# Row maxima spread through DRAM instead of by four transposes, in a fused cross-attention and feed-forward kernel

## The chip, the cores and the metric

The kernel runs on one core of one Trainium2 chip. The metric is the device time of one execution in microseconds. TensorE (PE) does the matrix products, VectorE (DVE), ScalarE (ACT) and GpSimd (POOL) the elementwise work, and SyncE (SP) starts transfers. Each engine works its own list of instructions in order; semaphores join them.

## The reference

There are B = 16 batches; each has x of 512 rows by 512 and a context c of 77 rows by 512.

```
h    = layernorm(x)
Sim  = (h@w1)[:,None] + (c@w2)[None,:] + (h*w3) @ c.T + b      # 512 x 77
A    = softmax(Sim, over the 77);   hq = A @ c
Batt = softmax(max(Sim, over the 77), over the 512 rows);  hbar = Batt @ h
x    = x + concat(h, hq, h*hq, h*hbar) @ W_qv + b_qv            # W_qv 2048 x 512
y    = layernorm(x) @ W1 + b1                                   # W1 512 x 2048
y    = y + (cos(th)*wr + sin(th)*wi) * 0.1 * wi * sin(th + 0.1*y)
x    = x + relu(y) @ W2 + b2                                    # W2 2048 x 512
```

## The kernel before

Every product is made of three TensorE passes on float32r operands split in a high and a low part (function `three`, lines L509 to L511): high by high, high by low, low by high. ScalarE makes the high part (a cast), VectorE the low part (a subtraction, `low`, L1061).

The work is a software pipeline written out by hand. `attention_first` (the opening) prepares the context products and does the attention of batch 0. Then `body(b, ...)` is run for b = 0 to 15, on each engine its own version. It does the feed-forward part of batch b in 16 steps f = 0 to 15 (one step is one 128-column block of W1 and the matching 128 rows of W2), and in between the attention part of the next batch, n = b + 1. In step f TensorE computes `hidden(b, f)` (12 matmuls into one of two `hid` buffers), and then `second(b, f - 3)` (12 matmuls into `acc`). `hidden(f)` may begin when ScalarE has read the same `hid` buffer (`h2_done` of step f - 2); `second(f - 3)` waits for `act_lo`, the low part that VectorE writes in `relu_low(f - 3)`. For each step ScalarE does `phase_and_hidden` (L866, L869), `relu_high` of the step before (L875) and `sine` (L879); VectorE does `reduce_phase` (L1202, L1204), `sine_term` (L1194) and `relu_low` of the step before (L1208). The pieces of the attention of batch n stand between these, each tied to a value of f. In b = 0 (called `first`) the weights are also split and stored, so each step carries `w1_high`, `w1_low`, `tile_high`, `tile_low` besides; later batches load the split weights again with DMAs from GpSimd.

The attention of batch n, in order: `g_high` and `g_low` (the context scaled by w3 plus w1, split); `spread_high` and `spread_low` (the normalized rows, split); `sim` (TensorE, f = 3, 12 matmuls into `mis[:, 0]`); `sim_bias` (ScalarE); `sim_rows` (four transposes, f = 4); `row_max` (VectorE: `rmax`, 128 x 4, one maximum for each of the 512 rows, f = 4); `spread_max` (TensorE, f = 5, L631: four transposes of a broadcast column of `rmax`, which put all 512 maxima in every partition of `mis[:, 0]`); `whole_max` (VectorE, L1228: their maximum `gmax`, f = 5); `max_exponentials` (ScalarE, L893: the exponentials into `e_bc` and their sum, f = 5); `probabilities`; `whole_prob_turn` (f = 6); `row_mean` (VectorE, L1267, four chunks: the weighted mean of the rows, two chunks at f = 6 and two at f = 7); `context_low` (f = 7); `w0_chunk` (VectorE, L1280, from f = 8), which needs the whole row mean; `hq_hat(0)` on TensorE at f = 9; and after `hidden(11)` the products of the attention, `products`, 16 groups of 12 matmuls whose operands come from `w0_low` and `chunk_low`. In `products` the first matmuls into `acc` wait for `add_first_part` (VectorE, L1304, f = 9), which empties it.

The row statistics of the next batch already go the way by DRAM (`spread_stats`, f = 12): TensorE turns a 128 x 12 tile with one transpose (`turn_stats`, L606), ScalarE copies it from PSUM (L796), SP stores it to `stat_dram` (L352), waits for that, and loads it with a broadcast into `mean_bc` and `e_bc` (L356).

SP's list in `body` is: the context loads at f = 0, the store of batch b - 1 at f = 4, the load of x for the batch after next at f = 6 (`x_load`, L342), `stack_low_in` at f = 7 (two small transfers into `at_s`, needed by `hq_hat(0)`), `turned_load` at f = 11, `spread_stats` at f = 12.

Of the kernel before, what the change touches and what calls it, by code (L numbers as in the profile page):

```python
# [31 lines left out]
ALU = mybir.AluOpType  # L32
# [5 lines left out]
P = 128  # L38
# [12 lines left out]
def xattn_ffn(nc, x, ctx_rows, w_sim, b_sim, W_qv, b_qv, W1, W2, b2, x_turned, ctx_turned, columns, out):  # L51
# [31 lines left out]
    wqx_dram = nc.dram_tensor("wqx_dram", [C, P, 2, D], F32).ap()  # L83
    stat_dram = nc.dram_tensor("stat_dram", [2, 3 * RT, P], F32).ap()
    hqw_dram = nc.dram_tensor("hqw_dram", [B * J, D], F32).ap()

    with ExitStack() as ctx:
# [76 lines left out]
        mv_x = row_x[:, 0:3].rearrange("p k t -> p t k")  # L164
        rmax = sb("rmax", [P, RT])
        rsum = sb("rsum", [P, RT])
        rrec = sb("rrec", [P, RT])
# [38 lines left out]
        exp_done = sem("exp_done"); rsum_done = sem("rsum_done"); rrec_done = sem("rrec_done")  # L206
        prob_done = sem("prob_done"); mbc_done = sem("mbc_done"); gmax_done = sem("gmax_done")
        ebc_done = sem("ebc_done"); erec_done = sem("erec_done"); at_done = sem("at_done")
# [127 lines left out]
        def _(sp):  # L336
# [12 lines left out]
            def spread_stats(n):  # L349
# [5 lines left out]
                for at, dst in ((0, mean_bc[:]), (2 * RT, e_bc[:])):  # L355
                    sp.dma_start(dst, stat_dram[n % 2, at:at + RT].rearrange("(a t) p -> a (t p)", a=1).to_broadcast([P, R])  # L356
                                 ).then_inc(bc_in, 16)

            def rows_in(k):

                need(sp, c_tlo, k - 3)
                m = chunk_rows(k)
                sp.dma_start(c_rows[k % 4][:, :, 0:m], ctx_turned[:, :, k * CR:k * CR + m]).then_inc(c_raw[k % 4], 16)
# [53 lines left out]
            def opening():  # L417
# [7 lines left out]
                rows_in(3)  # L425
                g_load(0, g0_in)
                stack_load(0, hq_raw, hq_tail, ctx_flat, hq0_in)
                rows_in(4)
                sp.dma_start(w2_bc[:], row(w_sim[D:2 * D], P)).then_inc(s_w2, 16)
                sp.dma_start(bsim[:], b_sim.rearrange("(a d) -> a d", a=1).to_broadcast([P, 1])).then_inc(s_bsim, 16)  # L430
                sp.dma_start(bqv_bc[:], row(b_qv, P)).then_inc(s_bqv, 16)
                rows_in(5)
# [33 lines left out]
            def body(b, par, first, last):  # L466
                n, pn = b + 1, 1 - par
                for f in range(FT):
# [10 lines left out]
                    if last:  # L479
                        continue  # L480
                    if f == NA - 3 and not first:
                        stack_low_in(n)
# [23 lines left out]
        def _(pe):  # L506
# [120 lines left out]
            def spread_max(n):  # L627

                pe.wait_ge(rmax_done, n + 1)
                for t in range(RT):  # L630
                    tr = pe.transpose(mis[:, 0, t * P:(t + 1) * P], rmax[:, t:t + 1].to_broadcast([P, P]), ident[:])  # L631
                tr.then_inc(mbc_done, 1)
# [150 lines left out]
        def _(sc):  # L783
# [103 lines left out]
            def row_exponentials(n):  # L887
                sc.wait_ge(shift_done, n + 1)
                nc.scalar.activation(prob[:], prob[:], ACT.Exp).then_inc(exp_done, 1)

            def max_exponentials(n):
                sc.wait_ge(gmax_done, n + 1)
                nc.scalar.activation(e_bc[:], mis[:, 0], ACT.Exp, bias=gmax[:], scale=1.0, accum_out=esum[:]  # L893
                                     ).then_inc(ebc_done, 1)
# [27 lines left out]
            def attention_first():  # L922
# [52 lines left out]
                product_copy(9)  # L975
                g_high(1)

            def body(b, par, first, last):
                n, pn = b + 1, 1 - par
                for f in range(FT):  # L980
# [32 lines left out]
                    if f == 0 and first:  # L1013
                        for c in range(C):
                            spread_high(n, c, pn)
                    if f == 1 and not first:
                        spread_high(n, 2, pn)
                        spread_high(n, 3, pn)
                        g_high(n)
                    if f == (4 if first else 2):  # L1020
                        context_high(n)
                    if f == 3 and not first:
                        sim_bias(n)
                    if f == 5:
                        max_exponentials(n)
# [25 lines left out]
        def _(ve):  # L1051
# [173 lines left out]
            def whole_max(n):  # L1225

                ve.wait_ge(mbc_done, n + 1)
                ve.tensor_reduce(gmax[:], mis[:, 0], AX.X, ALU.max, negate=True).then_inc(gmax_done, 1)  # L1228

# [116 lines left out]
            def attention_first():  # L1346
# [14 lines left out]
                low_part(3)  # L1361
                g_low(0)
                product_add(0)
                low_part(4)
                turned_low(0, 0, 0, full_done, t1_lo)
# [59 lines left out]
            def body(b, par, first, last):  # L1425
                n, pn = b + 1, 1 - par
                for f in range(FT):
# [25 lines left out]
                    if first and f < FT - 3:  # L1453
                        w1_low(f + 3)
                    if f == 0 and not first and not last:
                        scale(n, 0)
                        scale(n, 1)
                    if f == 0 and first:
                        g_low(n)
                        spread_low(n, 0, pn)  # L1460
                        spread_low(n, 1, pn)
                    if f == 1 and not last:
                        sim_column(n)
                        if first:
                            spread_low(n, 2, pn)
                            spread_low(n, 3, pn)
                        else:
                            spread_low(n, 0, pn)
# [12 lines left out]
                    if f == 5 and not last:  # L1481
                        whole_max(n)
                        probabilities(n)
                    if f == 6 and first:
                        prob_low(n)
                    if f == 6 and not last:
                        row_mean_scale(n)
                        row_mean(n, range(0, C // 2))
                    if f == 7 and not last:
                        row_mean(n, range(C // 2, C))  # L1490
                        context_low(n)
                    if f == NA - 2 and not last:
# [3 lines left out]
                    if first:  # L1496
                        for p in splits(f, last)[0:1] if f == NA else splits(f, last):
                            tile_low(p)
                    if f > 0 or not first:
                        relu_low(g - 1, (f - 1) % FT)  # L1500
# [202 lines left out]
```

## Time and profile before

| | us |
|---|---|
| three runs | 1960.26, 1960.32, 1960.84 (median 1960.32) |
| the profiled execution | 1960.47 |
| its span, first to last instruction | 1958.7 |

The view of engines gives busy time and share of the span. The timeline gives for each instruction its start, its duration, and in brackets the idle time before it with what ended that. TensorE's matmuls are pipelined: one lasts 0.39 us by its record, while the next starts about 0.23 us after it, so the distance between two starts is what one costs. The list of waits sums, for pairs of instructions, how long one engine stood idle for another. The granted clock is TensorE's, 1.00 for 2.4 GHz and 0.50 for 1.2 GHz.

### The profile page before, as it was taken

What the parts mean: (1) busy time and instruction counts of PE and PEld (TensorE: products, weight loads), DVE (VectorE), ACT (ScalarE), POOL (GpSimd) and SP (SyncE); (2) the same over time, 40 slices, a digit from 0 to 9 for tenths busy, and PEclk for the clock granted to TensorE, in tenths of its full rate; (3) what the DMA queues carried; (4) which work ended last, traced back from release to release, by engine and by line L of the source; (5) the groups of instructions that cost most, each with busy time, mean ns of one, the idle gap of its engine ahead of it and who ended that gap; (6) DMA issues with size and microseconds to landing.
All of it is one profiled execution on the core that took longest, in us unless ns stands there. A gap on an engine that the chain in (4) does not pass through costs nothing.

```text
span 1958.7 us, 24566 instructions
## 1 busy us (share of the span) xinstructions
PE 1940.7 (99%) x8751; PEld 1591.0 (81%) x8751; DVE 1378.9 (70%) x2377; ACT 985.6 (50%) x1662; POOL 388.9 (20%) x834
## 2 busy tenths in 40 slices
PE   8999999999999999999999999999999999999999
PEld 6778788888888888888888888888888888888887
DVE  7788776767677676776757767676776767767554
ACT  5475635536365363644636355363653636446343
POOL 1123221121211212112121211212112121121210
PEclk9999999999999999999999999999999999999999
DMA  8586847577574875757667475775747757475463
GB/s 258 161 294 233 280 143 232 175 221 221 160 228 143 247 220 165 237 152 223 198 197 223 145 237 163 232 220 159 238 138 240 222 170 232 146 225 183 150 211 123
DMA packets 142151, 393.93 MB, mean 201 GB/s; under 512 B 22100, under 2 KB 35080, under 8 KB 140110
## 3 DMA queue, kind: packets, MB, share of 16 engines
q0 software_dynamic: 83568, 304.29, 50.5%
q1 hardware_dynamic: 58318, 88.04, 14.5%
q8 instruction: 71, 1.16, 0.2%
q14 instruction: 50, 0.41, 0.1%
q10 hardware_dynamic: 144, 0.04, 0.0%
HBM read 351.83 MB, written 38.27 MB: 199 GB/s over the span
## 4 chain that ended last, share of the span: by engine, by line
PE 92%; DVE 3%; ACT 2%; issue 1%; DMA 1%; SPq 1%; DVEq 0%; ACTq 0%
PE acc L509 17%; PE acc L511 17%; PE acc L510 17%; PE hid L509 11%; PE hid L511 11%; PE hid L510 11%; PE mis L595 1%; PE acc L517 1%; PE acc L518 1%; PE mis L517 1%; PE mis L518 1%; PE mis L511 1%; PE mis L509 1%; PE mis L510 1%; DMA ctx_raw<-hqw_dram 0%
## 5 line engine op out<-in xcount | busy, mean ns | idle before, releaser
L509 PE MATMUL hid<-T,w1s 128*128 128x512 f32 x1024 | 403.6, 394 | 4.1 <-ACT h L869 4.0
L509 PE MATMUL acc<-ws,act 128*128 128x512 f32 x1024 | 402.8, 393 | 3.1 <-DVE act L1208 2.3
L510 PE MATMUL hid<-T,w1s 128*128 128x512 f32 x1024 | 399.7, 390 | 0.0
L511 PE MATMUL hid<-T,w1s 128*128 128x512 f32 x1024 | 399.6, 390 | 0.0
L511 PE MATMUL acc<-ws,act 128*128 128x512 f32 x1024 | 399.2, 390 | 0.0
L510 PE MATMUL acc<-ws,act 128*128 128x512 f32 x1024 | 398.8, 389 | 0.0
L1202 DVE TENSOR_SCALAR kk<-ph 128x512 f32<-128x512 f32 x256 | 108.7, 425 | 339.7 <-ACT ph L866 339.7
L875 ACT ACTIVATE act<-h 128x512 fp32r<-128x512 f32 x256 | 162.0, 633 | 350.6 <-DVE h L1194 329.2
L866 ACT ACTIVATE ph<-hid,hbias 128x512 f32<-128x512 f32 x256 | 175.6, 686 | 276.2 <-PE hid L511 275.8
L1559 POOL DMA_DIRECT2D ws<-w2x_dram x240 | 127.1, 530 | 558.1 <-PE acc L511 548.6
L509 PEld LDWEIGHTS hid<-T,w1s 128*128 128x128 f32 x1024 | 193.0, 188 | 45.6 <-issue 4.9
L1208 DVE SCALAR_TENSOR_TENSOR act<-h,act 128x512 fp32r<-128x512 f32 x256 | 176.0, 688 | 75.0 <-ACT act L875 73.0
L509 PEld LDWEIGHTS acc<-ws,act 128*128 128x128 f32 x1024 | 192.3, 188 | 43.3 <-DVE act L1208 4.2
L511 PEld LDWEIGHTS hid<-T,w1s 128*128 128x128 f32 x1024 | 192.8, 188 | 40.5
L511 PEld LDWEIGHTS acc<-ws,act 128*128 128x128 f32 x1024 | 192.2, 188 | 40.5
L510 PEld LDWEIGHTS hid<-T,w1s 128*128 128x128 f32 x1024 | 193.0, 188 | 38.7
L510 PEld LDWEIGHTS acc<-ws,act 128*128 128x128 f32 x1024 | 192.4, 188 | 38.9
L1553 POOL DMA_DIRECT2D w1s<-w1x_dram x240 | 129.2, 538 | 452.8 <-PE hid L511 440.9
L869 ACT ACTIVATE h<-hid,cols 128x512 f32<-128x512 f32 x256 | 174.1, 680 | 36.6 <-DVE act L1208 36.6
L1194 DVE SCALAR_TENSOR_TENSOR h<-ph,camp,h 128x512 f32<-128x512 f32 x256 | 190.9, 746 | 0.0
L1204 DVE TENSOR_TENSOR ph<-ph,kk 128x512 f32<-128x512 f32 x256 | 177.3, 693 | 8.8
L879 ACT ACTIVATE ph<-ph 128x512 f32<-128x512 f32 x256 | 158.2, 618 | 0.5
(186 smaller groups left out, 2694.0 us busy)
## 6 DMA issues: line engine op xcount, KB each, us to landing
w1s<-w1x_dram POOLq DMA_DIRECT2D x240, 512.0 KB, 4.4
ws<-w2x_dram POOLq DMA_DIRECT2D x240, 512.0 KB, 4.6
ws<-wqx_dram POOLq DMA_DIRECT2D x56, 512.0 KB, 3.6
full<-in_x_turned SPq DMA_DIRECT2D x15, 1024.0 KB, 8.1
out_x<-X SPq DMA_DIRECT2D x15, 1024.0 KB, 4.7
X<-in_x SPq DMA_DIRECT2D x14, 1024.0 KB, 8.1
w_raw<-in_L_ffn_W SPq DMA_DIRECT2D x32, 256.0 KB, 4.0
w1x_dram<-w1s POOLq DMA_DIRECT2D x16, 512.0 KB, 4.1
```

Source lines behind the costliest of these rows:

```text
L509: pe.matmul(dst, w_hi, m_hi, start=start, stop=False)
L510: pe.matmul(dst, w_hi, m_lo, start=False, stop=False)
L511: mm = pe.matmul(dst, w_lo, m_hi, start=False, stop=stop)
L866: nc.scalar.activation(ph[:, f % 2], hid[:, f % 2], ACT.Identity, bias=hbias[:, f:f + 1], scale=HSCALE).then_inc(t_done, 1)
L869: nc.scalar.activation(h2[:, f % 2], hid[:, f % 2], ACT.Identity, bias=b1c[:, f:f + 1], scale=1.0).then_inc(h2_done, 1)
L875: nc.scalar.activation(act[:, f % 4, 0], h2[:, f % 2], ACT.Relu).then_inc(act_hi, 1)
L879: nc.scalar.activation(ph[:, f % 2], ph[:, f % 2], ACT.Sin, scale=TWO_PI_BELOW).then_inc(s_done, 1)
L1194: ve.scalar_tensor_tensor(out=h2[:, f % 2], in0=ph[:, f % 2], scalar=camp[:, f:f + 1], in1=h2[:, f % 2], op0=ALU.mult, op1=ALU.add).then_i ...
L1204: ve.tensor_tensor(ph[:, f % 2], ph[:, f % 2], kk[:], ALU.subtract).then_inc(r_done, 1)
L1208: ve.scalar_tensor_tensor(out=act[:, f % 4, 1], in0=h2[:, f % 2], scalar=0.0, in1=act[:, f % 4, 0].bitcast(F32), op0=ALU.max, op1=ALU.subtract
L1553: po.dma_start(w1s[:, s].rearrange("p a c k -> p (a c k)"), w1x_dram[f % FT].rearrange("p a c k -> p (a c k)")).then_inc(w1_in[s], 16)
L1559: po.dma_start(ws[:, slot_of(p)], tile_source(p, last, w2x_dram, wqx_dram)).then_inc(w_in[slot_of(p)], 16)
```

## The change

For batches n > 1 the four transposes of `spread_max` become one, of the 128 x 4 tile `rmax` into four partitions of `mis[:, 0]`. ScalarE copies these to SBUF (`row_max_out`, f = 5), SP stores them to DRAM and loads them with a broadcast into `e_bc` (`spread_row_max`, f = 5). `whole_max` now waits for that load and reads `e_bc`; it moves from f = 5 to f = 6, `max_exponentials` too (in place in `e_bc`), and the `row_mean` halves to f = 7 and f = 8. For n = 0 and 1 the transposes stay.

In the opening, the load of the bias b_qv is started before the stacked context loads, and on VectorE `low_part(4)` goes ahead of `product_add(0)`. `g_high(1)` moves from the end of ScalarE's opening to the end of step 0 of b = 0, `g_low(1)` on VectorE from step 0 to step 1. In steps 5 to 9 of b = 0 `relu_low` goes directly behind `w1_low`, ahead of the attention pieces and `tile_low`.

```diff
+    rmax_dram = nc.dram_tensor("rmax_dram", [2, RT, P], F32).ap()
+        rrow = mean_bc[0:RT, 0:P]
...
@@ SP
+            def spread_row_max(n):
+                sp.wait_ge(rrow_done, n - 1)
+                sp.dma_start(rmax_dram[n % 2], rrow).then_inc(rbc_in, 16)
+                sp.wait_ge(rbc_in, 32 * (n - 1) - 16)
+                sp.dma_start(e_bc[:], rmax_dram[n % 2].rearrange("(a t) p -> a (t p)", a=1).to_broadcast([P, R])
+                             ).then_inc(rbc_in, 16)
...
                 g_load(0, g0_in)
+                sp.dma_start(bqv_bc[:], row(b_qv, P)).then_inc(s_bqv, 16)
                 stack_load(0, hq_raw, hq_tail, ctx_flat, hq0_in)
                 rows_in(4)
...
-                sp.dma_start(bqv_bc[:], row(b_qv, P)).then_inc(s_bqv, 16)
                 rows_in(5)
...
                     if last:
                         continue
+                    if f == 5 and not first:
+                        spread_row_max(n)
                     if f == NA - 3 and not first:
                         stack_low_in(n)
@@ TensorE, spread_max
                 pe.wait_ge(rmax_done, n + 1)
+                if n > 1:
+                    pe.transpose(mis[0:RT, 0, 0:P], rmax[:], ident[:]).then_inc(mbc_done, 1)
+                    return
@@ ScalarE
+            def row_max_out(n):
+                sc.wait_ge(mbc_done, n + 1)
+                nc.scalar.copy(rrow, mis[0:RT, 0, 0:P]).then_inc(rrow_done, 1)
...
-                nc.scalar.activation(e_bc[:], mis[:, 0], ACT.Exp, bias=gmax[:], scale=1.0, accum_out=esum[:]
+                nc.scalar.activation(e_bc[:], e_bc[:] if n > 1 else mis[:, 0], ACT.Exp, bias=gmax[:], scale=1.0, accum_out=esum[:]
...
                 product_copy(9)
-                g_high(1)
...
                     if f == 0 and first:
                         for c in range(C):
                             spread_high(n, c, pn)
+                        g_high(n)
...
-                    if f == 5:
+                    if f == 5 and not first:
+                        row_max_out(n)
+                    if f == (5 if first else 6):
                         max_exponentials(n)
@@ VectorE, whole_max
-                ve.wait_ge(mbc_done, n + 1)
-                ve.tensor_reduce(gmax[:], mis[:, 0], AX.X, ALU.max, negate=True).then_inc(gmax_done, 1)
+                if n > 1:
+                    ve.wait_ge(rbc_in, 32 * (n - 1))
+                else:
+                    ve.wait_ge(mbc_done, n + 1)
+                ve.tensor_reduce(gmax[:], e_bc[:] if n > 1 else mis[:, 0], AX.X, ALU.max, negate=True).then_inc(gmax_done, 1)
...
                 g_low(0)
+                low_part(4)
                 product_add(0)
-                low_part(4)
...
+                    early = first and 5 <= f < NA
+                    if early:
+                        relu_low(g - 1, f - 1)
...
                     if f == 0 and first:
-                        g_low(n)
                         spread_low(n, 0, pn)
                         spread_low(n, 1, pn)
...
                             spread_low(n, 3, pn)
+                            g_low(n)
...
                     if f == 5 and not last:
-                        whole_max(n)
+                        if first:
+                            whole_max(n)
                         probabilities(n)
...
-                    if f == 6 and not last:
+                    if f == 6 and not first and not last:
+                        whole_max(n)
+                    if f == (6 if first else 7) and not last:
                         row_mean_scale(n)
                         row_mean(n, range(0, C // 2))
                     if f == 7 and not last:
+                        context_low(n)
+                    if f == (7 if first else NA - 2) and not last:
                         row_mean(n, range(C // 2, C))
-                        context_low(n)
...
-                    if f > 0 or not first:
+                    if (f > 0 or not first) and not early:
                         relu_low(g - 1, (f - 1) % FT)
```

## Rows read from the trace of the kernel before

**Rows 1.** The page: busy time, share of the span and count, by engine

```profile
PE 1940.7 (99%) x8751; PEld 1591.0 (81%) x8751; DVE 1378.9 (70%) x2377; ACT 985.6 (50%) x1662; POOL 388.9 (20%) x834
```

**Rows 2.** Waits of TensorE over the whole run: total us, times, longest

```profile
PE hid L509 <- ACT h L869: 4.0, 1, 4.0
PE acc L509 <- DVE act L1208: 2.3, 2, 1.6
...
PE mis L517 <- ACT at_s L905: 0.9, 1, 0.9
```

**Rows 3.** Timeline of TensorE around the four transposes of a middle batch: start, duration

```profile
350.49 0.39 PE L511 MATMUL hid<-T,w1s 128*128 128x512 f32 x1
350.71 0.60 PE L631 MATMUL mis<-ident,rmax 128*128 128x128 f32 x4
351.07 0.48 PE L509 MATMUL acc<-ws,act 128*128 128x512 f32 x1
351.38 0.39 PE L510 MATMUL acc<-ws,act 128*128 128x512 f32 x1
```

**Rows 4.** The same around the single transpose of the row statistics

```profile
299.38 0.27 PE L606 MATMUL mis<-ident,row_x 128*12 128x128 f32 x1
...
299.72 0.40 PE L510 MATMUL hid<-T,w1s 128*128 128x512 f32 x1
```

**Rows 5.** Timeline of SP: statistics stored, then loaded; first and last of 13

```profile
299.97 0.33 SPq L352 DMA_DIRECT2D stat_dram<-mean_bc  x1
302.12 0.34 SPq L356 DMA_DIRECT2D mean_bc<-stat_dram  x1
...
1723.82 0.33 SPq L352 DMA_DIRECT2D stat_dram<-mean_bc  x1
1727.32 0.34 SPq L356 DMA_DIRECT2D mean_bc<-stat_dram  x1
```

**Rows 6.** Landing of the load into mean_bc (one tile's view, from 240 us on)

```profile
DMA to landing us min/median/max: 3.3/4.0/5.1
```

**Rows 7.** The page: the load issued just behind it (count, KB, median to landing)

```profile
e_bc<-stat_dram SPq DMA_DIRECT2D x15, 256.0 KB, 7.0
```

**Rows 8.** Timeline of ScalarE, step 5 of a middle batch

```profile
355.42 0.63 ACT L879 ACTIVATE ph<-ph 128x512 f32<-128x512 f32 x1
```

**Rows 9.** Timeline of TensorE, end of steps 6 and 9 of the same batch

```profile
356.62 0.60 PE L637 MATMUL mis<-ident,prob 128*77 128x128 f32 x4
...
376.13 0.39 PE L517 MATMUL mis<-at_s,hqs 128*128 128x512 f32 x1
```

**Rows 10.** Timeline of VectorE, steps 6 and 10 of the same batch

```profile
362.01 0.69 DVE L1208 SCALAR_TENSOR_TENSOR act<-h,act 128x512 fp32r<-128x512 f32 x1
...
383.06 0.69 DVE L1061 TENSOR_TENSOR prs<-full,prs 128x512 fp32r<-128x512 f32 x1
```

**Rows 11.** Timeline of VectorE, before and in step 0 of b = 0

```profile
76.57 2.48 DVE L1087 TENSOR_TENSOR full<-full,e_bc 128x1024 f32<-128x1024 f32 x2
...
85.12 0.47 DVE L1061 TENSOR_TENSOR gs<-tmp_w,gs 128x308 fp32r<-128x308 f32 x1
```

**Rows 12.** Timeline of ScalarE, steps 0 and 1 of b = 0

```profile
80.86 1.48 ACT L833 ACTIVATE tmp_w<-tmp_w,cols 128x77 f32<-128x77 f32 x4 [5.92 <-DMA ctx_raw<-hqw_dram]
...
82.72 0.68 ACT L866 ACTIVATE ph<-hid,hbias 128x512 f32<-128x512 f32 x1
...
85.16 2.17 ACT L791 CAST T<-full 128x512 fp32r<-128x512 f32 x4
87.22 0.68 ACT L866 ACTIVATE ph<-hid,hbias 128x512 f32<-128x512 f32 x1
```

**Rows 13.** Stretches: PE, PEld, DVE, ACT, POOL busy (count), granted clock, DMA share, GB/s

```profile
84.00:89.00 5.00, 4.88 (x12) 3.85 (x13) 3.92 (x7) 4.85 (x9) 0.53 (x1) 0.50 0.49 174
```

**Rows 14.** Timeline of VectorE, opening

```profile
19.09 0.69 DVE L1157 TENSOR_TENSOR X<-acc,bqv_bc 128x512 f32<-128x512 f32 x1 [1.92 <-DMA bqv_bc<-in_L_xattn_b_qv]
```

**Rows 15.** Timeline of TensorE: hq_hat(0) of b = 0, step 9

```profile
136.35 0.50 PE L517 MATMUL mis<-at_s,hqs 128*128 128x512 f32 x1 [0.89 <-ACT at_s L905]
```

More of the change, by code:

```diff
@@ L206, in xattn_ffn @@
         exp_done = sem("exp_done"); rsum_done = sem("rsum_done"); rrec_done = sem("rrec_done")
-        prob_done = sem("prob_done"); mbc_done = sem("mbc_done"); gmax_done = sem("gmax_done")
+        prob_done = sem("prob_done"); mbc_done = sem("mbc_done"); rrow_done = sem("rrow_done"); rbc_in = sem("rbc_in"); gmax_done = sem("gmax_done")
         ebc_done = sem("ebc_done"); erec_done = sem("erec_done"); at_done = sem("at_done")
```

## The prediction

> **What bounds the kernel now.** I read the busy times first: TensorE is busy 99% of the span, the others 70% or less [rows 1]. So the end is set by TensorE's own work, plus the few places where it stands still. The list of its waits says how few these are: about 14 us in all, each once or twice, none periodic; the three that the argument needs are in [rows 2]. The timeline puts every one before 226 us, that is in the opening, in b = 0 and at the start of b = 1. From there to the end TensorE has no gap. Two things can therefore make this kernel faster: less TensorE work in the steady batches, and shorter stalls before 226 us. Whatever the other engines do costs nothing unless it makes TensorE wait.
>
> **Part 1, the transposes.** With nothing between them, matmuls start 0.23 us apart. Around the four transposes the distance from the first transpose (350.71) to the second matmul behind them (351.38) is 0.67 us, where two starts further on would be 0.23: the four cost 0.67 - 0.23 = 0.44 us, 0.11 each [rows 3]. The single transpose of the row statistics has the form of the new one (a narrow weight of 12 columns, 128 columns streamed): 299.72 - 299.38 = 0.34, less 0.23, is 0.11 us [rows 4]. So a batch saves 0.44 - 0.11 = 0.33 us, and n = 2 to 15 are 14 batches: 4.6 us. It lies wholly on the path, if nothing new makes TensorE wait.
>
> **Part 2, the way round by DRAM.** The new chain replaces a result that was there at once. In a middle batch ScalarE ends the sine of step 5 at 355.42 + 0.63 = 356.05 [rows 8]. The copy out of PSUM has no row; the 128x308 operation of [rows 11] takes 0.47 us, so it lies between 0 and 0.47; I take 0.25, since a 4x128 tile is smaller: 356.3. Then SP stores 2 KB and waits. The nearest case is the statistics' store: 2.15 us from the store's issue to the load's in the first of 13 pairs, 3.50 in the last, the slowest [rows 5]; I take 2.1. The broadcast load of 256 KB lands 3.3 to 5.1 us after its issue, median 4.0 [rows 6], when it is the first in the queue, as here; the one behind it takes 7.0 [rows 7]. With 4.0 the maxima are there at 356.3 + 2.1 + 4.0 = 362.4, a round trip of 6.1 us.
>
> Who waits: VectorE comes to `whole_max` in step 6. TensorE ends hidden(6) where the transposes of rows 9 start, 356.62, now 0.3 earlier, and reduce_phase and sine_term of step 6 take some 2.5 us behind it, so VectorE is there at about 359 and stands for 3.4 us (TensorE does not; VectorE is idle 30% of the time [rows 1]). Queued behind it are relu_low(5) and all of step 7. `whole_max` lasts 0.6 us, so relu_low(5) starts at 363.05 where it started at 362.01 [rows 10]: 1.0 us late. ScalarE's exponentials wait for `gmax`, and phase_and_hidden(7) for them, about 0.7 us later than before. Two of the four row_mean chunks (0.8 us each) now stand in step 8, ahead of w0_chunk, and what was removed from step 6 was spent in the wait. So from step 8 on VectorE is 1.8 us late; the low part of the first product chunk, 383.06 before, starts at 384.9 and ends at 385.5 [rows 10]. TensorE wants it behind hq_hat(0) (376.13), 2 + 24 + 2 + 8 + 12 matmuls later, 48 x 0.229 = 11.0: 387.1, now 386.8 [rows 9]. Margin 1.3 us. The other meeting points (relu_low(6) for second(6), the emptying of `acc`) come out with 1.6 and 1.7. So the round trip may be 6.1 + 1.3 = 7.4 us before TensorE feels it. At the slow ends, 3.50 + 5.1 = 8.6 [rows 5, 6], it costs 1.2 us in that batch; at the fast end nothing. I take 0 as the sum and up to 2 us in all for stray slow ones.
>
> SP's queue: `x_load` (1 MB) now stands behind the maxima's round trip and starts some 13 us later; its rows are wanted in step 10, over 25 us on. stack_low_in finds it issued ahead of it, and `hq_hat(0)` at 376 needs those two small transfers; I see about 3 us of room. Nothing for either.
>
> The Trainium skill (DMA: Bandwidth & Descriptors, "Anatomy of one DMA") gives a transfer a fixed cost of about 2.0 us, most of it the receipt, plus its bytes at 436 GB/s. An estimate by that page: 2.0 + 2.0 + 0.6 = 4.6 us, 1.5 less than the 6.1 of the rows, and the rival of the slow round trip below would have no chance; the rows disagree, even in their first pair and fastest landing (2.15 + 3.3), so it keeps one.
>
> **Part 3, b = 0.** The largest stall, 4.0 us, is hidden(2) waiting for ScalarE's step 0 [rows 2], and ScalarE stood in `g_high(1)` until the context transfers landed at 80.86 [rows 12]. With `g_high` gone from there, ScalarE reads the first `hid` buffer at about 77.4 and hidden(2) runs at once. But the gap does not vanish. hidden(3) needs step 1's phase_and_hidden, and ahead of that stand now: VectorE's scaling until 76.57 + 2.48 = 79.05 [rows 11], reduce_phase 1.15, the sine 0.6 [rows 8], the four casts of spread_high 2.05, and g_high 82.72 - 80.86 = 1.86 [rows 12]. The sum is 84.7, against 87.22 before: 2.5 us earlier. VectorE's step 1 gains this, less 0.4 for `g_low`, which it takes on (0.47 by its record [rows 11]): 2.1. TensorE stalls again, 82.6 to 86.1, before hidden(3).
>
> From there until step 9 ScalarE and VectorE are the bound: TensorE lives on its lead and loses it, which is why it waits for `act` (2.3) and for `at_s` (0.9) at the end [rows 2]. The early relu_low takes the waits for `act` away: low parts 5 and 6 come 3 to 5 us sooner. But the cast into `at_s`, at the same place in ScalarE's list, moves by the 2.1 us only, less 0.1. So hq_hat(0), 136.35 before [rows 15], starts at about 134.3, with TensorE idle some 2.8 us in front of it: what the early relu_low gives turns into waiting there. Behind it relu_low(8) now fills an idle 0.6 us of VectorE ahead of the emptying of `acc`, and the small stalls there shrink: in all 2.2 us, between 1.3 (TensorE at half clock before `sim`) and 3.0. Until 226 us TensorE leads and the gain is carried whole.
>
> **Part 4, the opening.** VectorE idles 1.92 us for b_qv [rows 14]; TensorE waits behind it. Without that wait and with low_part(4) in it, the next low parts come 0.75 us sooner; but the 256 KB of b_qv now go ahead of `rows_in(4)`, which low_part(4) needs, and no row prices that: it can take back all of the 0.75 and a little more. Between -0.2 and 0.75: I take 0.3, the middle.
>
> **Sum.** 4.6 + 2.2 + 0.3 = 7.1 us. The profiled execution took 1960.47 (span 1958.7), 0.15 over the median of the runs; 1960.47 - 7.1 = 1953.4, as a median 1953.2. A measurement of this kernel tells 0.2% (3.9 us) from no change, so "faster" is below 1956.4.
>
> **The rivals.**
>
> *The clock falls at the new stall.* After the idle before 84.12 the granted clock was 0.50 (1.2 GHz) [rows 13], and there 12 matmuls cost 0.43 instead of 0.23 us each, 2.4 us. The same behind the 2.8 us before hq_hat(0) would lie on the path: 1953.2 + 2.4 = 1955.6. For it: the idle time is nearly as long as 4.0. Against: it is shorter by a third. The Trainium skill (TensorE: Matmul & The Clock Gate, "What's actually happening") has half clock as the default and activity as what lifts it; by that rule this is the outcome, and [rows 13] agree after the longer idle.
>
> *The round trip uses a third of a microsecond per batch.* At a mean of 7.7 us TensorE loses 0.3 x 14 = 4.2 us, nearly the transposes: 1957.4, no change. For it: the spread of rows 5. Against: medians give 6.1.
>
> *The round trip is the bound: slower.* If the load lands as the second one did, 2.1 + 7.0 = 9.1 us [rows 5, 7], VectorE passes 1.7 us of it on in every batch: 14 x 1.7 = 23.8, less 7.1: 1977. It decides from 7.4 + 7.1 / 14 = 7.9 us. For it: weight loads of 512 KB run beside it. Against: there is no transfer ahead of it in SP's queue.
>
> *All stalls of b = 0 go.* If the chain of ScalarE and VectorE shortens as well, another 4 us: 1949.
>
> **How the numbers follow.** Forecast 0.52, clock 0.20, a third per batch 0.10, slower 0.10, all stalls 0.08. Faster is the forecast, the last one, and 0.17 of the clock's: 0.77. Same is the third per batch and the rest of the clock's: 0.13. Slower 0.10. The range runs from 1950 (b = 0 and the opening at their best ends, 1.3 more, and half of the last rival's rest) to 1958.3 (past the clock and the third per batch); it leaves out slower and most of the last.
>
> **What would show it.** After 226 us TensorE still without waits, a batch's period 0.33 us shorter (before, the 13 statistics stores of [rows 5] stand (1723.82 - 299.97) / 12 = 118.65 apart): part 1. One transpose of 0.27 us per batch at `spread_max`. VectorE waiting 2 to 4 us for the DMA into `e_bc` in step 6: part 2; TensorE waiting for `prs`, `act` or `acc` in each batch would refute it. In b = 0: stall of about 3.4 us before hidden(3) and 2 to 3 us before hq_hat(0), none for `act`: part 3. VectorE without wait for b_qv: part 4. The forecast is wrong if the steady period does not shrink, or if b = 0 gains less than 1 or more than 4 us.

## The result and the profile after

| | us |
|---|---|
| before, 11 runs | median 1960.76 (1960.15 to 1962.54) |
| after, 11 runs | median 1956.02 (1954.32 to 1959.05) |
| ratio | 0.9976, 95% interval 0.9968 to 0.9984 |
| the profiled executions | 1960.47 before (span 1958.7), 1955.15 after (span 1953.3) |

The change saves 4.7 us in the medians and 5.3 us between the profiled executions; 7.1 was forecast. The interval of the ratio is 3.1 to 6.3 us. The direction is as forecast, the saving is two thirds of the forecast one. The spread is new: 2.4 us between the fastest and the slowest run before, 4.7 after.

The page of the changed kernel, busy times by engine, beside [rows 1]: TensorE has 42 matmuls less, three for each of 14 batches.

```profile
PE 1938.4 (99%) x8709; PEld 1585.8 (81%) x8709; DVE 1379.2 (71%) x2377; ACT 990.4 (51%) x1676; POOL 408.4 (21%) x834
```

The waits of TensorE over the whole run, beside [rows 2] (total, times, longest):

```profile
PE hid L521 <- ACT h L884: 3.3, 1, 3.3
PE acc L521 <- DVE act L1082: 1.9, 1, 1.9
...
PE acc L521 <- DVE ws L1082: 1.5, 2, 0.9
PE mis L529 <- DVE hqw L1082: 0.9, 1, 0.9
PE mis L529 <- ACT at_s L924: 0.8, 1, 0.8
PE acc L521 <- DVE X L1328: 0.7, 1, 0.7
```

The waits for `act` of `relu_low` are gone, and waits for the weight tiles `ws` have come. TensorE's timeline where the transposes stood, beside [rows 3]:

```profile
348.26 0.39 PE L523 MATMUL hid<-T,w1s 128*128 128x512 f32 x1
348.48 0.27 PE L643 MATMUL mis<-ident,rmax 128*4 128x128 f32 x1
348.51 0.48 PE L521 MATMUL acc<-ws,act 128*128 128x512 f32 x1
348.83 0.40 PE L522 MATMUL acc<-ws,act 128*128 128x512 f32 x1
```

348.83 - 348.48 = 0.35 instead of 0.67 us. The period of a batch can be read from SP's timeline:

```profile
946.07 0.25 SPq L364 DMA_DIRECT2D rmax_dram<-mean_bc  x1
...
1064.40 0.25 SPq L364 DMA_DIRECT2D rmax_dram<-mean_bc  x1
```

It is 118.33 us, 0.32 below the 118.65 of before. But not all are: between the transposes of the row statistics (L618 now) the periods of the batches are 118.54, 118.33, 118.33, 118.56, 118.33, 118.33, 118.33, 118.34, 118.70, 118.33, 118.33, 118.56. TensorE's timeline shows where a long one loses its 0.2 us, at the last emptied accumulator:

```profile
380.91 0.39 PE L529 MATMUL acc<-hqw,at_s 128*128 128x512 f32 x1
381.14 0.39 PE L530 MATMUL acc<-hqw,at_s 103*128 103x512 f32 x1
381.38 0.50 PE L529 MATMUL acc<-hqw,at_s 128*128 128x512 f32 x1
381.71 0.40 PE L530 MATMUL acc<-hqw,at_s 103*128 103x512 f32 x1
```

The start after 381.38 comes 0.33 us later instead of 0.23, and most of the rest is lost in the next ten microseconds in smaller steps. Such a pause is too short to be listed as idle; it shows only in the distance between starts. What makes it is on the other engines, in the same batch of the changed kernel. ScalarE's timeline, the copy of the row maxima (start, duration):

```profile
353.74 0.24 ACT L908 COPY mean_bc<-mis 4x128 f32<-4x128 f32 x1
```

SP's timeline, the store, the broadcast load and the load of x behind it:

```profile
354.00 0.25 SPq L364 DMA_DIRECT2D rmax_dram<-mean_bc  x1
355.30 0.34 SPq L366 DMA_DIRECT2D e_bc<-rmax_dram  x1
355.68 0.43 SPq L344 DMA_DIRECT2D X<-in_x  x1
```

VectorE's timeline, the reduction that waits for the load, and the emptying of `acc` (in brackets the idle time before):

```profile
361.19 0.69 DVE L1252 TENSOR_REDUCE gmax<-e_bc 128x1 f32<-128x512 f32 x1 [4.41 <-DMA e_bc<-rmax_dram]
...
378.85 2.47 DVE L1328 TENSOR_TENSOR X<-X,acc 128x512 f32<-128x512 f32 x4
```

The round trip, from the end of the copy (353.98) to 361.19, took 7.2 us. The store took 1.3 of it, the load 5.9. VectorE's waits for it sum to 56.1 us in 14 batches, 4.0 each. The last of the four emptyings ends at 381.3, and TensorE wanted that accumulator at 381.4: the margin is used up.

This batch is one of the slow ones. Read in the same way in all 14, the round trip is 7.15 to 7.4 us in five batches (n = 2, 3, 6, 11 and 14) and 6.6 to 6.9 in the eight others up to n = 14. The long periods are those of the five: they lose 0.2 to 0.4 us each, the eight lose nothing. (For n = 2 the period is 120.17 us, against 119.80 in e3 below, which has no such loss.) In the last batch (n = 15) no load of x follows, and the load is there 3.7 us after its issue, where the others took 5.3 to 6.1:

```profile
1776.34 0.34 SPq L366 DMA_DIRECT2D e_bc<-rmax_dram  x1
```

and VectorE's reduction there:

```profile
1780.02 0.69 DVE L1252 TENSOR_REDUCE gmax<-e_bc 128x1 f32<-128x512 f32 x1 [2.25 <-DMA e_bc<-rmax_dram]
```

In b = 0 and at the start of b = 1, four rows of TensorE's timeline mark the way: the last stall of the opening, then before hidden(3), before hq_hat(0), and before the first `second` of b = 1.

```profile
37.71 0.47 PE L529 MATMUL mis<-at_s,hqs 128*128 128x512 f32 x1 [0.88 <-DVE hqw L1082]
...
86.11 0.77 PE L521 MATMUL hid<-T,w1s 128*128 128x512 f32 x1 [3.25 <-ACT h L884]
...
134.42 0.50 PE L529 MATMUL mis<-at_s,hqs 128*128 128x512 f32 x1 [0.84 <-ACT at_s L924]
...
218.03 0.47 PE L521 MATMUL acc<-ws,act 128*128 128x512 f32 x1 [0.73 <-DVE X L1328]
```

The same two places, first and last, in the kernel before:

```profile
37.59 0.47 PE L517 MATMUL mis<-at_s,hqs 128*128 128x512 f32 x1 [0.87 <-DVE hqw L1061]
...
220.34 0.47 PE L509 MATMUL acc<-ws,act 128*128 128x512 f32 x1 [0.73 <-DVE X L1304]
```

This splits the 5.4 us of span: the opening 37.59 against 37.71, -0.1; from there to the start of b = 1, 182.75 against 180.32, 2.4; the rest, 1958.7 - 220.34 against 1953.3 - 218.03, 1738.4 against 1735.3, 3.1.

### The profile page after: what moved, and what is told of

Its sections match the earlier page's. It is cut to its first block, busy times and chain, and to the rows that moved or that the text cites. A ratio compares the mean times of both kernels' runs of the same rounds, so it can differ in the third digit from the quotient of the medians.

```text
span 1953.3 us, 24524 instructions
## 1 busy us (share of the span) xinstructions
PE 1938.4 (99%) x8709; PEld 1585.8 (81%) x8709; DVE 1379.2 (71%) x2377; ACT 990.4 (51%) x1676; POOL 408.4 (21%) x834
## 4 chain that ended last, share of the span: by engine, by line
PE 93%; DVE 3%; ACT 2%; issue 1%; DMA 0%; SPq 0%; DVEq 0%; ACTq 0%
PE acc L521 18%; PE acc L523 17%; PE acc L522 17%; PE hid L521 11%; PE hid L523 11%; PE hid L522 11%; PE mis L607 1%; PE acc L529 1%; PE mis L529 1%; PE acc L530 1%; PE mis L530 1%; PE mis L523 1%; PE mis L521 1%; PE mis L522 1%; DVE ph L1225 0%
```

## The experiments

Eleven kernels were run, with five rounds each (e5 three). e1 to e4 shared one set of runs of the kernel before (median 1961.26), e5 to e8 another (1961.58), e9 to e11 a third (1961.20). For each trace the three parts above are read: end of the opening, the distance from it to the stall near 218 us, and the rest of the span.

| | median us | ratio to before, 95% | opening ends | distance | rest of span |
|---|---|---|---|---|---|
| e1 way by DRAM only | 1958.18 | 0.9979 to 0.9996 | 37.50 | 182.74 | 1735.0 |
| e2 b = 0 and opening only | 1958.21 | 0.9979 to 0.9997 | 39.00 | 180.30 | 1738.3 |
| e3 load of x first | 1954.18 | 0.9952 to 0.9977 | 37.98 | 180.44 | 1733.9 |
| e4 copy early | 1954.40 | 0.9956 to 0.9980 | 38.06 | 180.30 | 1733.8 |
| e5 second store | 1996.65 | 1.0160 to 1.0191 | 39.52 | 180.40 | 1779.0 |
| e6 e3, g back | 1956.18 | 0.9964 to 0.9984 | 37.82 | 182.68 | 1733.8 |
| e7 e3, relu_low late | 1954.74 | 0.9956 to 0.9981 | 39.64 | 180.60 | 1733.9 |
| e8 e3, opening back | 1955.23 | 0.9956 to 0.9981 | 39.36 | 180.35 | 1733.9 |
| e9 e3 and e4 | 1953.77 | 0.9953 to 0.9977 | 37.78 | 180.25 | 1733.8 |
| e10 e9, opening back | 1953.66 | 0.9952 to 0.9977 | 37.63 | 180.31 | 1733.9 |
| e11 e9, g later | 1952.52 | 0.9946 to 0.9971 | 37.73 | 179.09 | 1733.8 |

The kernel before had 1960.76 beside the changed kernel and 1961.20 to 1961.58 in these sets, so medians of different sets are not to be compared to a few tenths. Each against the kernel before of its own set, the changed kernel saves 4.7 us, e3 7.1, e4 6.9, e6 5.4, e7 6.8, e8 6.4, e9 7.4, e10 7.5 and e11 8.7.

**e1 and e2, each half alone.** e1 takes the opening and b = 0 back, e2 the way by DRAM.

> Only the way by DRAM (one transpose, store, broadcast load, row means at steps 7 and 8); the opening and b = 0 as before. My theory: the period between two statistics stores falls by 0.33 us in a batch whose round trip is short, and by 0.0 to 0.3 where it is over some 7.2 us, the lack standing as small gaps of TensorE at the first matmuls of the attention products; nothing before 226 us changes. In all 2.5 to 4.6 us less than the kernel before, and a larger spread between runs than the kernel before has. Rival, that the transposes are hidden anyway: no change. Rival, that the gain of the whole change is from b = 0: no change here.

> Only the edits of the opening and of b = 0; the four transposes stay in every batch. My theory: 2.2 to 2.5 us less than the kernel before, read at the stall that both show near 220 us, which comes at about 218.0; the spread between runs is that of the kernel before. The rival, that the way by DRAM brings all of the gain: no change.

Measured: 3.1 us less with either, in the medians. e1 changes nothing before 220 us (stall at 220.24), saves 3.4 us in the rest, loses 0.1 to 0.4 us in five batches, those whose round trip is 7.1 to 7.5 us, and spreads from 1956.9 to 1961.9. e2 saves 2.45 us in the distance; its spread is 2.3 us. In the parts of the traces the two halves add up (3.4 and 2.45 us, against 3.1 and 2.4 together in the changed kernel); the medians, 6.1 against 4.7, are too rough to show it, since each half's interval is some 3 us wide. The greater spread belongs to the way by DRAM.

**e3, the load of x first.**

```diff
                     if f == 5 and not first:
+                        if n + 1 < B:
+                            x_load(n + 1)
                         spread_row_max(n)
...
-                    if f == 6 and not first:
-                        x_load(n + 1)
```

> The changed kernel with SP's 1 MB load of x put ahead of the store of the maxima in its list, where it starts some 10 us before them. My theory: the broadcast load took 5.9 us to land where 4.0 was expected because the 1 MB load is issued 0.4 us behind it and shares the 16 queues; with the queue to itself it lands in 3.5 to 4.5 us, VectorE waits about 3 us instead of 4.0 to 4.4 per batch, the gaps at the attention products vanish and the median is 1 to 2 us under the changed kernel. The rival, that the weight loads from GpSimd or the memory set the landing: 5.5 us or more, and no change of the time.

Measured, SP's timeline in e3:

```profile
342.94 0.40 SPq L344 DMA_DIRECT2D X<-in_x  x1
354.02 0.26 SPq L364 DMA_DIRECT2D rmax_dram<-mean_bc  x1
355.33 0.34 SPq L366 DMA_DIRECT2D e_bc<-rmax_dram  x1
```

and VectorE's reduction in the same batch of e3:

```profile
358.84 0.69 DVE L1252 TENSOR_REDUCE gmax<-e_bc 128x1 f32<-128x512 f32 x1 [2.04 <-DMA e_bc<-rmax_dram]
```

The load is there 3.5 us after its issue instead of 5.9. This batch shows the greatest difference: over the batches n = 2 to 14 the load takes 3.3 to 4.8 us, 4.1 in the mean, instead of 5.3 to 6.1, 5.6 in the mean. VectorE's waits fall from 56.1 to 37.3 us in all, every period after the first affected batch is 118.33 to 118.35, and the five runs lie between 1953.7 and 1954.5. The theory holds: a transfer of 1 MB issued 0.4 us behind the broadcast load slowed it by 1.5 us in the mean, and that used up VectorE's margin. The last batch of the changed kernel, which has no load of x behind it and took 3.7 us, says the same. That the two share the queues is the theory's reason; no run separates it from others.

**e4, the copy early.** ScalarE's `row_max_out` stands directly behind phase_and_hidden of step 5; the load of x stays where the change put it.

```diff
                     phase_and_hidden(b, f)
+                    if f == 5 and not first and not last:
+                        row_max_out(n)
...
-                    if f == 5 and not first:
-                        row_max_out(n)
```

> The changed kernel with ScalarE's copy of the maxima directly behind phase_and_hidden of step 5, ahead of relu_high, a table load and the sine. TensorE's transpose ends 5 us before the copy starts in the changed kernel, so the store starts about 3.8 us sooner. My theory: VectorE's wait for the load falls from 4.0 to under 1 us in each batch, relu_low and the emptying of the accumulators come back to their old place, no gap is left after 226 us in TensorE, every period is 118.33 us, and the median is 1 to 3 us under the changed kernel with a spread like the kernel before. The rival, that the small gaps come from the moved row means and not from the round trip: the gaps stay and the time is that of the changed kernel.

Measured, SP's timeline in e4:

```profile
350.02 0.25 SPq L364 DMA_DIRECT2D rmax_dram<-mean_bc  x1
352.49 0.34 SPq L366 DMA_DIRECT2D e_bc<-rmax_dram  x1
```

and VectorE's in e4:

```profile
358.47 0.69 DVE L1252 TENSOR_REDUCE gmax<-e_bc 128x1 f32<-128x512 f32 x1 [1.76 <-DMA e_bc<-rmax_dram]
```

The load still takes 5.3 to 6.1 us in the batches with the load of x behind it, but all starts 4 us sooner. The wait is 1.3 us on average (18.7 in all; under 1 was expected), no gap is left, and the time is that of e3. Two remedies of different kinds give the same 4.5 us in the rest of the span: what counts is when the maxima are there, not which part of the trip is short. The moved row means, which both keep, cost TensorE nothing.

**e5, a second store.** The opposite: SP stores the maxima twice, with a wait between.

```diff
                 sp.dma_start(rmax_dram[n % 2], rrow).then_inc(rbc_in, 16)
-                sp.wait_ge(rbc_in, 32 * (n - 1) - 16)
+                sp.wait_ge(rbc_in, 48 * (n - 1) - 32)
+                sp.dma_start(rmax_dram[n % 2], rrow).then_inc(rbc_in, 16)
+                sp.wait_ge(rbc_in, 48 * (n - 1) - 16)
```

> The changed kernel with the store of the maxima made twice, one after the other with a wait between, which lengthens the round trip by one store, 1.2 to 1.6 us, and changes nothing else. My theory: the round trip of 7.2 us stands just at the point where TensorE begins to wait, so all that is added comes out again in every batch: periods of 119.5 to 119.8 us instead of 118.33 to 118.7, the gaps at the emptying of the accumulators and the product chunks, and 14 x 1.3 = 18 us more, about 1974 us. The rival, that the small gaps are matter of the moved row means or of TensorE's own issue: the time stays within 2 us of the changed kernel's.

Measured: 1996.65, 40.6 us over the changed kernel where 18 were expected. The mechanism is as expected, the added trip is not. In the trace of e5 VectorE's waits for the load sum to 97.2 us, 6.9 per batch, so the second store added 2.9 us and not 1.3. TensorE waits in every batch, for `act` and not first for `acc`. The waits of TensorE in e5 (total, times, longest):

```profile
PE acc L523 <- DVE act L1231: 24.7, 15, 1.9
```

and one of them in TensorE's timeline of e5:

```profile
378.02 0.50 PE L523 MATMUL acc<-ws,act 128*128 128x512 f32 x1 [1.71 <-DVE act L1231]
```

In 7 of the 14 batches the stall was followed by half clock. In one of them a matmul at 500.72 starts 0.43 us after the one before, and the windows view of e5 gives for that stretch (its length, the busy times of PE, PEld, DVE, ACT and POOL with counts, the granted clock, the DMA share and GB/s):

```profile
499.80:503.20 3.40, 3.40 (x8) 2.72 (x9) 3.15 (x9) 1.74 (x3) 0.00 (x0) 0.50 0.55 169
```

The periods separate clock and round trip. In the six other batches up to n = 14 the round trip is 9.5 to 9.9 us and the period 2.5 to 2.9 us over 118.33: just what the round trip has over 7.0 us. In the seven with half clock the period is 3.7 to 4.3 us over it (for n = 2, over 119.80), 0.9 to 1.0 more than their round trip over 7.0, which makes some 7 us. So the profiled execution (2000.81 us, the slowest of four) is 45.7 us over that of the changed kernel: about 37 from the round trip, 7 from the clock, 2 from a late opening. That 14 x 2.9 = 41 comes so near to the 40.6 between the medians is in part chance: the median executions have a clock share too, and their traces were not kept. What the run shows for the change is the slope: past a round trip of 7.0 us TensorE pays all that is added, and sometimes the clock on top.

**e6, g_high and g_low back.**

```diff
                 product_copy(9)
+                g_high(1)
...
                             spread_high(n, c, pn)
-                        g_high(n)
```

(and `g_low(n)` from step 1 to step 0 on VectorE).

> The kernel of e3 (x load first) with g_high(1) back at the end of ScalarE's opening and g_low(1) back in step 0. My theory: the stall of 4.0 us before hidden(2) is back, the stall near 218.4 us comes 2.2 to 2.4 us later counted from the stall near 38 us (182.7 instead of 180.4 us apart), and the median is 2.3 us over e3. The rival, that the early relu_low carries the gain of b = 0: under 1 us.

Measured: the stall before hidden(2) is back, 4.14 us at 84.42; the distance is 182.68 against 180.44, 2.24 us more, and the median 2.0 more (1.7 against the kernel before of each set). All but 0.1 to 0.2 us of what b = 0 gained is the move of g_high.

**e7, relu_low late.** `early = False`.

> The kernel of e3 with relu_low of b = 0 back behind the attention pieces in all steps. My theory: TensorE waits for act again, once or twice before step 9 (1.6 and 0.7 us), and then less or nothing for the weight tiles and for at_s; the distance from the stall near 38 us to the one near 218 us grows by 0.2 us or less, 0.3 us of the median at most. The rival, that relu_low early is what shortens b = 0: 2 us.

Measured: TensorE waits for `act` again, 0.46 and 0.70 us; the distance is 0.16 us longer. The median is 0.56 over e3, but the kernel before was 0.32 higher in this set too, so some 0.2 is left, as expected. The profiled execution is 1.8 us over that of e3, and 1.7 of this is the opening: it ended at 39.64, and the granted clock was low in it. The windows view of e7, with columns as for e5:

```profile
21.00:25.00 4.00, 3.41 (x13) 2.84 (x14) 2.06 (x4) 2.42 (x6) 0.00 (x0) 0.64 0.57 161
```

**e8 and e10, the opening back.** The b_qv load and the order of `product_add(0)` and `low_part(4)` as before the change, on the base of e3 and of e9.

> The kernel of e3 with the b_qv load and the order of low_part(4) and product_add(0) as before the change. In the traces with the new opening the last stall of the opening ends at 37.71, 37.98, 38.06 and 39.00 us, in the two with the old one at 37.50 and 37.59. My theory now: the load moved ahead delays the context rows by more than it gives, so the old opening ends at 37.5 to 37.6 and the median is 0.3 to 0.8 us under e3. The rival, my forecast of 0.3 us for the new opening: the median is 0.3 us over e3.

> As e9, with the opening of the kernel before (b_qv load late, product_add(0) ahead of low_part(4)). My theory: the two orders are equal within 0.5 us of the median, and what moves the end of the opening (37.5 to 39.6 us in the traces so far) is whether the granted clock falls to 0.50 around 22 to 25 us. The rivals: 0.3 us over e9 (my forecast for the new opening), or 0.3 to 0.8 us under it (the load moved ahead holds the context rows up).

Measured: e8 came out 1.05 us over e3 (0.7 against the kernel before of each set), which would speak for the new opening; but its trace has the low clock at 21 to 25 us too (0.60), and its opening ended at 39.36, like that of e5 and e7, which have the new one. e10, run beside e9 with full clock in both traces, is 0.1 us under it, and its opening ends 0.15 sooner. The medians of the two orders are equal within what can be measured, so the harm of 0.3 to 0.8 us written down for e8 is not confirmed. In the traces, though, the new order is never the sooner one: with full clock at 21 to 25 us the old opening ends at 37.50 to 37.63 (before, e1, e10) and the new one at 37.71 to 38.06 (the changed kernel, e3, e4, e6, e9, e11); with half clock there the old one ends at 39.36, the new one at 39.52 and 39.64. The clock is not all that moves it either: e2 ended its opening at 39.00 at full clock. What made that one late was not followed up.

**e9, both remedies.**

> Both remedies: the load of x first in SP's list (e3) and ScalarE's copy directly behind phase_and_hidden of step 5 (e4). My theory: the store starts at about 350 us, the load lands 3.5 us after its issue, VectorE does not wait for it in most batches (under 0.5 us), all periods 118.33 us; since TensorE has no gap in e3 or in e4 either, the time is theirs, 1953.7 to 1954.6 us. The rival, that a shorter wait of VectorE is worth something by itself: 1 us or more under e3.

Measured: the waits for the load fall to 6.9 us in all, the time to 1953.77, the same as e3. VectorE's idle time is worth nothing once TensorE has no gap.

**e11, g_high later.** On the base of e9.

```diff
-                        g_high(n)
...
                     sine(b, f)
+                    if f == 1 and first:
+                        g_high(n)
```

> As e9, with g_high(1) moved once more, from the end of step 0 to behind the sine of step 1. My theory, that from step 1 to step 9 the pair ScalarE and VectorE is the bound: the stall before hidden(3) shrinks from 3.2 us to about 1.4 and the clock may stay full there, but TensorE waits the same 1.8 us more later, at sim, for act, for the weight tiles or for at_s, and the distance between the last stall of the opening and the one near 218 us stays at 180.1 to 180.7 us; the time is that of e9. The rival, that the stall before hidden(3) is itself the bound: 1.5 to 1.9 us less.

Measured, TensorE's timeline of e11 before hidden(3) and sim:

```profile
84.25 0.47 PE L521 MATMUL hid<-T,w1s 128*128 128x512 f32 x1 [1.35 <-ACT h L884]
...
88.98 0.45 PE L521 MATMUL mis<-T,gs 128*77 128x512 f32 x1 [1.73 <-DVE gs L1083]
```

and VectorE's of e11 at the start of step 2:

```profile
90.18 0.42 DVE L1224 TENSOR_SCALAR kk<-ph 128x512 f32<-128x512 f32 x1
```

The stall before hidden(3) shrinks as expected, and the one at sim grows from 1.17 us in e9 to 1.73. But the time falls by 1.25 us, to 1952.52, and the distance by 1.2. My expectation of none was wrong, and the rival's 1.5 to 1.9 is not reached. VectorE's step 2 starts at 90.18; in e9 it starts at 91.41:

```profile
91.41 0.42 DVE L1223 TENSOR_SCALAR kk<-ph 128x512 f32<-128x512 f32 x1
```

That is 1.23 us sooner, and from there to 222 us VectorE, ScalarE and TensorE stay 1.0 to 1.4 us ahead of e9, most of the time 1.2. This is the gain. The pair is the bound, as the theory had it; what it had wrong is that g_high costs the pair 1.86 us wherever it stands. In step 1 a part of it lies beside VectorE's own work, in ScalarE's idle time. e11 is the fastest of all: its median is 3.5 us under that of the changed kernel.

## Why the prediction came out as it did

Between the profiled executions the span is 5.4 us shorter where 7.1 were forecast: 4.5 from the transposes (4.6 forecast), 1.4 lost again on the way by DRAM (0), 2.4 in b = 0 (2.2), and 0.1 lost in the opening (0.3 gained). The median, 1956.02, lies nearer to the numbers of two rivals (1955.6 and 1957.4) than to 1953.2. For the clock rival that is chance, since its mechanism did not happen; the rival of a third of a microsecond per batch named the mechanism that did.

**Part 1, 4.6 us: right.** One transpose costs 0.11 to 0.12 us and a batch saves 0.32 to 0.33. With the gaps taken away, the rest of the span shortens by 1738.4 - 1733.9 = 4.5 us (e3, e4, e9).

**Part 2, nothing lost: the term that was mis-sized.** The step was "a round trip of 6.1 us" and, of `x_load`, "Nothing for either". In the batch shown it took 7.2 us: the store 1.3 for the 2.1 taken, the load 5.9 for 4.0. In the mean of the batches n = 2 to 14 it took 7.0: the store 1.3, the load 5.6. The row of 4.0 [rows 6] had a 256 KB load behind it; here a 1 MB load stood there, and in e3, without it, the load took 4.1 in the mean. So the two terms were off by 0.8 and 1.6 us in opposite directions, and it is luck that the sum was only some 0.9 us short. I looked at whether x would come in time, and not at what it would do to the transfer ahead of it. The consequence for VectorE was argued rightly: it waited 4.0 us (3.4 forecast). The limit was not. It was given as 7.4 us, at the product chunk; TensorE began to lose at 7.0, at `acc`. The 1.7 us given as the margin of the emptying of `acc` holds for the first of the four accumulators only. The kernel before shows it, first and last of the four in TensorE's timeline:

```profile
382.54 0.40 PE L517 MATMUL acc<-hqw,at_s 128*128 128x512 f32 x1
...
383.94 0.40 PE L517 MATMUL acc<-hqw,at_s 128*128 128x512 f32 x1
```

and VectorE's emptying of all four:

```profile
378.03 2.47 DVE L1304 TENSOR_TENSOR X<-X,acc 128x512 f32<-128x512 f32 x4
```

TensorE asks for the next one every 0.47 us, VectorE empties one in 0.6. The last is free at 378.03 + 2.47 = 380.50, with the forecast delay of 1.8 us at 382.3, and wanted at 383.94 - 0.33 = 383.6: a margin of 1.3 us, no more than at the product chunk. Where the other 0.4 between 7.4 and 7.0 went was not followed up.

In the profiled execution this cost 1.4 us of the 4.5. It was in the bounds ("up to 2 us in all") and in the rival of a third of a microsecond per batch: the truth of this trace is 0.1 per batch. The runs lie within 4.7 to 5.0 us of each other with the gaps (the changed kernel, e1) and within 0.8 to 2.4 without them (e3, e4, e6 to e11), so the greater spread belongs to them too. That the median run lost more than the profiled one for the same reason is likely, but not shown: one trace of it was kept.

The 4.6 us that the prediction estimates by the Trainium skill (DMA: Bandwidth & Descriptors, "Anatomy of one DMA") rests on a fit that the section states for transfers issued by GpSimd; these are SP's. The trace comes near that estimate only in the last batch, with 1.4 + 3.7 = 5.1 us; in the others it does not agree.

**Part 3, 2.2 us: right, 2.4 measured.** Forecast and found: hidden(3) at 86.1 (86.11), stall 3.4 (3.25), hq_hat(0) at 134.3 (134.42), no wait for `act`. Not found: 2.8 us of idle time before hq_hat(0). It was 0.84, because TensorE already waited for `ws` (0.56 and 0.93), whose low parts now stand behind relu_low. So the time that relu_low gave was spent in two other waits before it reached hq_hat(0), and its worth is 0.16 us (e7). The rival of the clock did not happen where it was placed: the stall before hq_hat(0) was 0.84 us, and the granted clock stayed at 1.00 behind it. After the 3.25 us before hidden(3) it did read 0.50 in the changed kernel, and in e9 it stayed at 1.00, with the same distance to 218 us. That part has slack for TensorE, as the chain of ScalarE and VectorE is the bound.

**Part 4, 0.3 us: not confirmed.** VectorE no longer waits for b_qv, and the opening ends 0.1 us later. e10 puts the difference of the medians at nothing, and no trace shows the new order ahead.

**The slow rival** (1977) failed in the change, but e5 shows it was a real one: 2.9 us more of round trip give 1996.65, some of it by the clock.

That e3 saves 7.1 us against the kernel before of its set is the forecast number by chance, and not by its parts: its trace is 4.5 us shorter in the rest of the span and 2.3 in b = 0, and its opening 0.4 longer.

## What to carry to other kernels

On an engine at 99%, count first what leaves that engine's list; then find the other engine's margin to it, because a detour by DRAM is free only while it fits. When a transfer is put on a path with little margin, look at what is issued right behind it in the same list, and not only ahead: here that alone cost 1.5 us of landing in the mean, and 2.4 in the worst batch. Start such a detour as soon as its data are there; the producer's copy stood 5 us behind the transpose for no reason but its place in ScalarE's list.

## What the runs showed of the hardware

- A broadcast load of 256 KB was there 3.3 to 4.8 us after its issue with no 1 MB load behind it (e3; 3.7 in the last batch of the changed kernel) and 5.3 to 6.1 with a 1 MB load issued 0.4 us later (the changed kernel, e4).
- A 2 KB store to DRAM, from its issue to the next one behind the wait, took 1.2 to 1.6 us in the changed kernel, and 2.2 to 2.5 in e4, when it was issued 4 us sooner. Repeated at once it took 2.5 to 3.0 us, after 1.2 to 1.4 for the first (e5; issues at 359.31, 360.75 and 363.37 in one batch). Why is not shown.
- The same stall of about 3.2 us before hidden(3) was followed by half clock in the changed kernel, e3, e4, e5, e7 and e8, and by full clock in e2, e9 and e10. In e5 the nine stalls of 1.82 to 1.95 us in the steady batches were followed by half clock seven times; the shorter ones (1.73 us and less) never were. In the opening, the clock fell around 8 to 12 us in the traces of e5, e7 and e8 and again around 22 to 26, and each of these openings ended some 1.7 us later than the others of its order; e4, with the first fall alone, ended it at 38.06. The windows view of 86 to 91 us, with columns as for e5, of the changed kernel:

```profile
86.00:91.00 5.00, 4.89 (x12) 3.86 (x13) 4.96 (x11) 2.72 (x5) 0.53 (x1) 0.50 0.38 129
```

and of e9:

```profile
86.00:91.00 5.00, 3.66 (x15) 2.67 (x16) 4.96 (x11) 2.78 (x6) 0.53 (x1) 1.00 0.37 124
```

The granted clock is 0.50 in the one and 1.00 in the other, and TensorE is busy for 4.89 us with 12 matmuls at the low clock, for 3.66 with 15 at the full one.
